# Row maxima over every second query, written to memory as two pieces of 16 bytes

## The chip, the cores and the metric

The kernel runs on one core of a Trainium2 chip. Its engines work side by side: TensorE (PE; its weight loads are listed apart, as PEld), VectorE (DVE), ScalarE (ACT), GpSimd (POOL) and the queue of SyncE (SP), which here issues nearly all transfers. The metric is the device time of one execution in microseconds, and a kernel's time is the median of several runs.

## What is computed

Two layers over x of 4 batches x 1024 tokens x 128 features. The change touches the attention of the first layer alone:

```python
qkv = X @ W_qkv                                   # 16 heads of 64, for q, k and v
q, k, v = (qkv[..., 0], qkv[..., 1], qkv[..., 2])
scores = jnp.einsum('bqhd,bkhd->bhqk', q, k) / scale
weights = jax.nn.softmax(scores, axis=-1)
attn = jnp.einsum('bhqk,bkhd->bqhd', weights, v)
return attn.reshape(b, s, h * d) @ W_out
```

A layer norm and a router of experts come ahead of it, the experts behind it, and then the second layer (a decaying recurrence and a gated network with weights rounded to 4 bits).

## The kernel before

Attention (`layer0_attention`) goes over N = 32 visits: 4 batches by 8 pairs of heads. The two heads of a pair lie on partitions 0 to 63 and 64 to 127 of `q_hi`, `k_hi` (the rounded parts of q and k) and `q_lo`, `k_lo` (the rests). The scores are made transposed: a tile has 128 keys as its partitions and the 512 queries of one half of the tokens, for both heads, as its columns. A visit has 16 steps t: half hf = t // 8, key tile kt = t % 8.

Softmax wants each query's maximum over all keys taken off ahead of the exponential. In the transposed tile a query is a column, and so the maxima come in another way:

- `row_max` on TensorE makes the scores once more, coarsely, the other way round: the queries are the stationary operand, 512 keys the moving one. One call is two matmuls, one for each head, into the bank pair `ps_m`. The 512 queries of a half are taken in four groups. A group is every fourth query, so the weight load (L1285) reads 128 fp32 columns of `q_hi` with a step of four elements, 16 bytes.
- `row_max` on VectorE (L1549) reduces `ps_m` to one maximum per query and head, in `mxh`. After eight such (4 groups by 2 halves of the keys) L1554 joins the key halves in `mx`: 8 numbers per partition.
- `spread` on the SP queue writes `mx` to the memory tensor `peaks` (L1169; a partition's 8 numbers, 32 bytes, are one run there), waits, and reads the 1024 numbers back to all 128 partitions, into `peak[hf]` (L1171).
- `seed` (L1455 on ScalarE; two steps of a visit, t = 3 and 15, L1681 on VectorE) writes minus the peak to a bank pair of `ps_s`, and `scores` (L1301, six matmuls a step: k_hi by q_hi, k_lo by q_hi, k_hi by q_lo, for two heads) adds upon it. L1471 takes the exponential on ScalarE into `probs`, a ring of 8; GpSimd adds the tiles up for the denominators (L1530).

All order is written out by hand. TensorE does two steps in a row, called a pair here, and each pair holds: row_max, the scores of the two steps, row_max, one item (a projection of K, Q or V for the next visit at L1232 to L1251, or an output projection, L1271), the products with V of two earlier steps (`values`, L1310) and, in two of the eight pairs of a visit, the sum for the denominators (L1260). `row_max` is 12 tiles ahead of the scores, so the eighth tile of a half is reduced at t = 3 or t = 11, and its peak is first wanted by the seed of t = 8 or of t = 0 of the next visit. `ps_m` is one bank pair: a call of row_max waits (m_done) for VectorE's reduction of the one before. ScalarE's pair is: two exponentials, the read of the item (L1418, L1424, or L1427 for a denominator), two seeds, and some small work (L1439 keep_values, L1409 stage, L1405, L1434). The seed of step t waits for the exponential of t - 2, which reads the same banks; `scores` waits for the seed.

Of the kernel before, what the change touches and what calls it, by code (L numbers as in the profile page):

```python
# [4 lines left out]
F32 = mybir.dt.float32  # L5
# [3 lines left out]
ALU = mybir.AluOpType  # L9
ACT = mybir.ActivationFunctionType  # L10
AX = mybir.AxisListType
# [3 lines left out]
P = 128  # L15
# [20 lines left out]
def attention_early(nc, ctx, g):  # L36

    sb, pb, sem = g.scope(ctx)
    g.qkv = sb("qkv_raw", [P, 3, PAIRS, 2 * DH], F32)
    g.wout = sb("wout_raw", [P, PAIRS, D], F32)  # L40
    g.w_hi = sb("w_hi", [P, 2, 2 * DH], F32R)
    g.w_lo = sb("w_lo", [P, 2, 2 * DH], F32R)
    g.wv_hi = sb("wv_hi", [P, PAIRS, 2 * DH], F32R)
    g.wv_lo = sb("wv_lo", [P, PAIRS, 2 * DH], F32R)
    g.wo = [sb("wo0", [P, D], F32), g.wo_last]
    g.probs = sb("probs", [P, RING, 2, CH], F32)
    g.psum_k = [sb(f"psum_k{h}", [P, 2, CH], F32) for h in range(2)]
    g.place = sb("place", [P, 2, TILES], U32)
    g.ones = sb("ones", [P, DH], F32)
    g.mx = sb("mx", [P, 4, 2], F32)  # L50
    g.V = [sb(f"V{p}", [P, TPB, 2 * DH], F32) for p in range(2)]

    spare = g.psum_k[0][:, :, :].rearrange("p x c -> p (x c)")
    g.top_i = spare[:, 0:256].bitcast(U32).rearrange("p (t e) -> p t e", e=E)
    g.carry = spare[:, 256:512].rearrange("p (e t) -> p e t", e=E)
    g.before = spare[:, 512:640]
    g.ones_n = spare[:, 640:768]
    g.ratio = spare[:, 768:768 + TILES]
    g.iota8 = spare[:, 800:800 + E]
    g.tile_no = spare[:, 808:808 + ROUTED]  # L60
    g.row_no = spare[:, 840:841]
    g.attn_w_in = sem("attn_w_in")
    g.preset = sem("preset")
    g.w_staged = sem("w_staged")
    g.wlo_staged = sem("wlo_staged")
    g.add_done = sem("add_done")
# [301 lines left out]
def load_rows(nc, sp, g, tile, s):  # L368

    dst = g.x_raw[s].rearrange("p (t d) -> p t d", d=ROW)  # L370
    sp.dma_start(dst, g.rows[bass.ds(tile * CH, CH), :].rearrange("(n p) d -> p n d", p=P)).then_inc(g.x_tile_in[s], 16)


def load_weights(nc, sp, g, first, w, s):

    sp.dma_start(w.bitcast(F32), g.w_split[bass.ds(first, P), :]).then_inc(g.w_tile_in[s], 16)
# [606 lines left out]
def layer0_attention(nc, ctx, g):  # L983

    sb, pb, sem = g.scope(ctx)
# [16 lines left out]
    probs, psum_k, ones, mx, V = g.probs, g.psum_k, g.ones, g.mx, g.V  # L1002
    w_in, preset, w_staged, wlo_staged, add_done = g.attn_w_in, g.preset, g.w_staged, g.wlo_staged, g.add_done
    even = [w[:, k * T:(k + 1) * T] for w in g.w_first for k in range(2)]
    k_hi, k_lo, q_hi, q_lo = ([even[k], sb(f"{name}1", [P, T], F32R)] for k, name in enumerate(("k_hi", "k_lo", "q_hi", "q_lo")))
# [5 lines left out]
    mxh = sb("mxh", [P, 2, 4, 2], F32)  # L1011
# [41 lines left out]
    mx_done = sem("mx_done")  # L1053
    mx_out = sem("mx_out")
# [47 lines left out]
    def max_bank(unit, i):  # L1102

        k = unit * KT + i if isinstance(unit, int) else KT + EARLY
        return ps_s[0] if k < KT + EARLY and k % 2 else ps_m

    def reads(n, name):

        c = READER[name]
        if n is None:  # L1110
            return sum(READER[k] == c for k in FIRST[:FIRST.index(name) + 1])
        if n is N:
            return N * PER[c] + AHEAD[c] + sum(READER[k] == c for k in LAST[:LAST.index(name) + 1])
        return n * PER[c] + AHEAD[c] + sum(READER[k] == c for k in LIST[:LIST.index(name) + 1])
# [32 lines left out]
    with nc.Block() as block:  # L1147
        @block.sync
        def _(sp):

            def move(p):

                sp.dma_start(V[p][:, :, :], V_next[:, :, p * 2 * DH:(p + 1) * 2 * DH]).then_inc(v_moved[p], 16)

            def expert_part(n):

                rows, col = bass.ds(n // QUARTERS * P, P), n % QUARTERS * QW
                sp.wait_ge(we_lo_done, n + 1)
                sp.dma_start(g.w_split[rows, bass.ds(col, QW)], we_hi[:, :].bitcast(F32)).then_inc(we_out, 16)
                sp.dma_start(g.w_split[rows, bass.ds(col + 2 * FF, QW)], we_lo[:, :].bitcast(F32)).then_inc(we_out, 16)  # L1160

            def load_part(n):

                sp.dma_start(we[:, :], g.inp["experts_d"][bass.ds(n // QUARTERS * P, P), bass.ds(n % QUARTERS * QW, QW)]).then_inc(we_in, 16)

            def spread(unit, hf):

                sp.wait_ge(mx_done, unit + 1)
                sp.dma_start(g.peaks[hf:hf + 1, :].rearrange("a (q k) -> q (a k)", k=8), mx[:, :, :].rearrange("p t x -> p (t x)")).then_inc(mx_out, 16)  # L1169
                sp.wait_ge(mx_out, unit * 16 + 16)  # L1170
                sp.dma_start(peak[hf][:, :, :].rearrange("p c x -> p (c x)"), g.peaks[hf:hf + 1, :].to_broadcast([P, 2 * CH])).then_inc(peak_in, 16)  # L1171

            load_part(0)
            spread(0, 0)
            sp.wait_ge(xa_done, AHEAD["a"])
            move(0)
            with sp.Fori(0, N // 2) as i:
                n = i * 2
                sp.wait_ge(v_ready, n * 2 + 1)
                move(1)  # L1180
                batch = bass.ds((n + 2) // PAIRS % B * T, T)
                sp.dma_start(xs_hi[:, :].bitcast(F32), g.xh[:, batch].bitcast(F32)).then_inc(xs_in, 16)
                sp.dma_start(xs_lo[:, :].bitcast(F32), g.xl[:, batch].bitcast(F32)).then_inc(xs_in, 16)
                spread(n * 2 + 1, 1)
                expert_part(n)
                load_part(n + 1)
                spread(n * 2 + 2, 0)
                spread(n * 2 + 3, 1)
                expert_part(n + 1)
                load_part((n + 2) % N)  # L1190
                spread(n * 2 + 4, 0)
                sp.wait_ge(xa_done, reads(n + 1, "V1"))
                move(0)
            sp.wait_ge(peak_in, (N * 2 + 1) * 16)
            sp.wait_ge(we_in, (N + 1) * 16)
            sp.wait_ge(we_out, N * 32)
            sp.wait_ge(v_moved[0], (N // 2 + 1) * 16)
            sp.wait_ge(scattered, 2 * TILES * 16)
            sp.wait_ge(routed, 2)
            load_rows(nc, sp, g, 0, 0)  # L1200
            sp.wait_ge(m_ready, KT + EARLY + N * STEPS)
            sp.wait_ge(xv_done, reads(N - 1, "Q1"))
            first = [sp.value_load(g.tile_w[0:1, s:s + 1], min_val=0, max_val=(E - 1) * P) for s in range(2)]
            load_weights(nc, sp, g, first[0], g.w_first[0][:, :], 0)
            load_rows(nc, sp, g, 1, 1)
            load_weights(nc, sp, g, first[1], g.w_first[1][:, :], 1)

        @block.tensor
        def _(pe):
# [64 lines left out]
            def row_max(unit, i, par, hf):  # L1274

                kh, t = divmod(i, 4)
                m = max_bank(unit, i)
                if m is ps_s[0] or isinstance(unit, int):
                    if unit * KT + i >= 2:
                        pe.wait_ge(m_done, unit * KT + i - 1)  # L1280
                else:
                    pe.wait_ge(m_done, unit * KT + i)
                q = q_hi[par][:, :].rearrange("p (c t) -> p t c", t=4)[:, t, hf * P:(hf + 1) * P]
                for x, rows in enumerate(HEADS):
                    ins = nc.tensor.matmul(m[:, x, :], q[rows, :], k_hi[par][rows, kh * CH:(kh + 1) * CH],  # L1285
                                           start=True, stop=True)
                ins.then_inc(m_ready, 1)
# [41 lines left out]
            def first_max(unit, *parts):  # L1329
                for i in parts:  # L1330
                    row_max(unit, i, 0, unit)
# [30 lines left out]
            for n, par in pairs(pe):  # L1362
                for t in range(STEPS):
                    p = t // 2
# [178 lines left out]
        def _(v):  # L1543
            def row_max(unit, i):
                kh, t = divmod(i, 4)
                v.wait_ge(m_ready, unit * KT + i + 1)
                if i == 0 and not (isinstance(unit, int) and unit == 0):
                    v.wait_ge(mx_done, unit)
                nc.vector.tensor_reduce(mxh[:, kh, t, :], max_bank(unit, i)[:, :, :], AX.X, ALU.max).then_inc(m_done, 1)  # L1549
                if i == KT - 1:  # L1550
                    v.wait_ge(m_done, unit * KT + KT)
                    if not (isinstance(unit, int) and unit == 0):
                        v.wait_ge(mx_out, unit * 16)
                    nc.vector.tensor_reduce(mx[:, :, :], mxh[:, :, :, :].rearrange("p k t x -> p t x k"), AX.X, ALU.max).then_inc(mx_done, 1)  # L1554

            def low(n, name, par):
                hi, lo = (k_hi, k_lo) if name[0] == "K" else (q_hi, q_lo)
# [939 lines left out]
```

## Time and profile before

| what | us |
|---|---|
| median of 3 runs | 1895.43 |
| lowest, highest | 1894.71, 1897.18 |
| the profiled execution | 1889.88 |
| its span, first to last instruction | 1888.0 |
| the attention's loop in it, about | 85 to 1485 |
| one visit in it | 43.78 |

The profiled execution is 5.5 us below the median. The profile gives, for an instruction, its start, its duration and, where its engine sat idle ahead of it, what ended that idle time. The ends of matmuls are modelled, so here starts are compared with starts. A weight load is a record of its own on PEld, and its matmul's record begins at the same moment where TensorE had stood still.

### The profile page before, as it was taken

To read this page: it belongs to the slowest core of one execution; us is meant where nothing else is said; L and a number is where in the kernel's file an instruction comes from. 1 tells how busy PE (TensorE), PEld (TensorE's weight loads), DVE (VectorE), ACT (ScalarE), POOL (GpSimd) and SP (SyncE) were. 2 spreads that over 40 slices of the span, in tenths; PEclk is the share of its full clock that TensorE was granted. 3 is DMA by queue.
4 is the path that set the end of the run, shared out by engine and by line. 5 is a ranking of instruction groups with operands and counts; after the bars stand their busy time and mean duration, and the time that the engine had idled before them with its cause. 6 is when DMAs were issued, how large, how long until landed. Compare 5 with 4: busy or idle time off the path is not lost. (4 is left out here: it accounts for less than half of the span.)

```text
span 1888.0 us, 32039 instructions
## 1 busy us (share of the span) xinstructions
PE 1785.0 (95%) x9247; PEld 989.1 (52%) x9247; DVE 1519.8 (80%) x2053; ACT 1464.2 (78%) x1954; POOL 1448.2 (77%) x868
## 2 busy tenths in 40 slices
PE   5799999999999999999999999999999899985687
PEld 4445444454454455554544544545445587763456
DVE  6787788888878777878878888778788788888896
ACT  4388888888888888888888888888888688874653
POOL 4288888888888888888888888888888457755564
PEclk9899999999999999999999999999999999997899
DMA  7112021212121121202121212112121577531000
GB/s 249 60 54 78 34 78 35 78 46 76 45 67 47 66 83 48 78 34 78 35 79 54 68 45 67 54 59 89 41 78 34 174 226 248 154 95 56 0 18 28
DMA packets 117014, 143.31 MB, mean 76 GB/s; under 512 B 18417, under 2 KB 98353, under 8 KB 113778
## 3 DMA queue, kind: packets, MB, share of 16 engines
q1 hardware_dynamic: 111986, 132.61, 22.4%
q0 software_dynamic: 4992, 10.27, 1.6%
q8 instruction: 16, 0.26, 0.1%
q14 instruction: 20, 0.16, 0.0%
HBM read 87.20 MB, written 27.64 MB: 61 GB/s over the span
## 5 line engine op out<-in xcount | busy, mean ns | idle before, releaser
L1530 POOL TENSOR_TENSOR psum_k<-psum_k,probs 128x1024 f32<-128x1024 f32 x384 | 929.9, 2422 | 144.8 <-ACT probs L1471 125.8
L1549 DVE TENSOR_REDUCE mxh<-ps_m 128x2 f32<-128x1024 f32 x518 | 623.6, 1204 | 242.7 <-PE ps_m L1285 242.6
L1471 ACT ACTIVATE probs<-ps_s 128x1024 f32<-128x1024 f32 x512 | 496.9, 1023 | 164.0 <-PE ps_s L1301 146.3
L1310 PE MATMUL ps_v<-probs,V 128*64 128x512 f32 x2056 | 494.6, 602 | 0.0
L1310 PEld LDWEIGHTS ps_v<-probs,V 128*64 128x64 f32 x2056 | 130.5, 136 | 239.2 <-issue 183.8
L1455 ACT ACTIVATE ps_s<-qkv_raw 128x1024 f32<-128x1024 f32 x224 | 243.6, 1124 | 0.0
L1455 ACT ACTIVATE ps_s<-peak 128x1024 f32<-128x1024 f32 x224 | 243.6, 1122 | 0.0
L1565 DVE RECIPROCAL e_y_row<-e_y_row 128x128 f32<-128x128 f32 x256 | 241.4, 943 | 0.0
L1530 POOL TENSOR_TENSOR psum_k<-probs 128x1024 f32<-128x1024 f32 x64 | 152.6, 2384 | 63.7 <-ACT probs L1471 47.7
L1301 PE MATMUL ps_s<-e_ew 64*128 64x512 f32 x1536 | 198.8, 390 | 0.0
L1285 PE MATMUL ps_m<-e_ew 64*128 64x512 f32 x524 | 163.9, 622 | 5.4 <-DVE mxh L1549 4.7
L1285 PEld LDWEIGHTS ps_m<-e_ew 64*128 64x128 f32 x524 | 80.9, 305 | 159.2 <-issue 104.6
L1301 PEld LDWEIGHTS ps_s<-e_ew 64*128 64x128 f32 x1536 | 146.3, 188 | 29.2 <-ACT ps_s L1455 2.4
L1285 PE MATMUL ps_m<-k_hi,q_hi 64*128 64x512 f32 x512 | 159.4, 619 | 0.0
L854 POOL DMA_INDIRECT results<-e_y_row,e_y_at x92 | 105.3, 1145 | 70.3 <-ACT e_y_row L795 43.4
L1285 PEld LDWEIGHTS ps_m<-k_hi,q_hi 64*128 64x128 f32 x512 | 79.0, 305 | 150.6 <-issue 103.8
L1301 PE MATMUL ps_s<-q_lo,k_hi 64*128 64x512 f32 x512 | 101.5, 392 | 0.0
L1301 PE MATMUL ps_s<-q_hi,k_lo 64*128 64x512 f32 x512 | 100.7, 389 | 0.0
L1301 PE MATMUL ps_s<-q_hi,k_hi 64*128 64x512 f32 x512 | 100.6, 389 | 0.0
L779 ACT ACTIVATE e_relu<-e_ps_z 128x512 f32<-128x512 f32 x124 | 74.6, 601 | 30.9 <-PE e_ps_z L708 28.3
L896 DVE TENSOR_TENSOR e_relu<-e_relu 128x512 f32<-128x512 f32 x108 | 74.5, 690 | 19.9 <-ACT e_relu L779 10.3
L900 DVE TENSOR_TENSOR e_h_lo<-e_relu,e_h_hi 128x512 fp32r<-128x512 f32 x124 | 88.4, 717 | 1.5 <-ACT e_h_hi L784 1.5
(317 smaller groups left out, 2918.0 us busy)
## 6 DMA issues: line engine op xcount, KB each, us to landing
e_ew<-w_split SPq DMA_DIRECT2D x23, 1024.0 KB
qkv_raw<-peaks SPq DMA_DIRECT2D x33, 512.0 KB, 3.9
V<-e_x_raw SPq DMA_DIRECT2D x33, 512.0 KB, 5.1
peak<-peaks SPq DMA_DIRECT2D x32, 512.0 KB, 4.1
xs_hi<-xh SPq DMA_DIRECT2D x16, 512.0 KB, 4.1
xs_lo<-xl SPq DMA_DIRECT2D x16, 512.0 KB, 5.0
rows<-in_blank_d SPq DMA_DIRECT2D x4, 1483.5 KB, 16.1
e_x_raw<-rows SPq DMA_DIRECT2D x23, 258.0 KB
```

The costliest lines, as they stand in the source:

```text
L779: nc.scalar.activation(r[:, q % NZ, :], ps_z[q % NZ][:, :], ACT.Relu).then_inc(relu_done, 1)
L854: nc.gpsimd.indirect_dma_start(g.results[:, :], bass.IndirectOffsetOnAxis(ap=y_at[s][:, t, 0:1], axis=0), y_row[s][:, t, :], None).then_in ...
L896: nc.vector.tensor_tensor(r2[:, q % NH, :], r[:, q % NZ, :], r[:, q % NZ, :], ALU.mult).then_inc(sq_done, 1)
L900: nc.vector.tensor_tensor(h_lo[:, q % NH, :], r2[:, q % NH, :], h_hi[:, q % NH, :].bitcast(F32), ALU.subtract).then_inc(lo_done, 1)
L1285: ins = nc.tensor.matmul(m[:, x, :], q[rows, :], k_hi[par][rows, kh * CH:(kh + 1) * CH], start=True, stop=True)
L1301: ins = nc.tensor.matmul(o[:, x, :], lhs[par][rows, keys], rhs[par][rows, qs], start=False, stop=True, skip_group_check=True)
L1310: ins = nc.tensor.matmul(ps_v[rows, :], V[par][:, kt, rows], probs[:, t % RING, x, :], start=kt == 0, stop=kt == KT - 1)
L1455: nc.scalar.activation(ps_s[t % 2][:, :, :], peak[hf][:, :, :].rearrange("p c x -> p x c"), ACT.Copy, scale=-1.0).then_inc(seeded, 1)
L1471: nc.scalar.activation(probs[:, t % RING, :, :], ps_s[t % 2][:, :, :], ACT.Exp, scale=SCALE).then_inc(p_done, 1)
L1530: nc.gpsimd.tensor_tensor(acc, probs[:, (t - 1) % RING, :, :] if kt == 1 else acc, probs[:, t % RING, :, :], ALU.add).then_inc(add_done, 1)
L1549: nc.vector.tensor_reduce(mxh[:, kh, t, :], max_bank(unit, i)[:, :, :], AX.X, ALU.max).then_inc(m_done, 1)
L1565: ins = nc.vector.reciprocal(rden[:, cols], den[:, cols])
```

## The change

The four groups of queries become two by two. The 512 queries of a half are split in two runs of 256 (s), and in each run a group is every second query (t). So L1285 loads 128 columns of `q_hi` with a step of two elements, 8 bytes, where it was four. `mx` holds the same 8 numbers per partition in the same order (group, head), named [s, t, x] now. Since the four numbers of s = 0 and those of s = 1 belong 2048 bytes apart in `peaks`, a partition's 32 bytes go there as two pieces of 16 bytes: 256 pieces where there were 128. `peaks` and `peak` look as before. Number, kind and order of the instructions on every engine stay the same.

```diff
-    g.mx = sb("mx", [P, 4, 2], F32)
+    g.mx = sb("mx", [P, 2, 2, 2], F32)
...
                 sp.wait_ge(mx_done, unit + 1)
-                sp.dma_start(g.peaks[hf:hf + 1, :].rearrange("a (q k) -> q (a k)", k=8), mx[:, :, :].rearrange("p t x -> p (t x)")).then_inc(mx_out, 16)
+                sp.dma_start(g.peaks[hf:hf + 1, :].rearrange("a (s q k) -> q (a s) k", s=2, k=4), mx[:, :, :, :].rearrange("p s t x -> p s (t x)")).then_inc(mx_out, 16)
...
-                q = q_hi[par][:, :].rearrange("p (c t) -> p t c", t=4)[:, t, hf * P:(hf + 1) * P]
+                two = hf * 2 + t // 2
+                q = q_hi[par][:, :].rearrange("p (c t) -> p t c", t=2)[:, t % 2, two * P:(two + 1) * P]
...
-                    nc.vector.tensor_reduce(mx[:, :, :], mxh[:, :, :, :].rearrange("p k t x -> p t x k"), AX.X, ALU.max).then_inc(mx_done, 1)
+                    nc.vector.tensor_reduce(mx[:, :, :, :].rearrange("p s t x -> p (s t) x"), mxh[:, :, :, :].rearrange("p k t x -> p t x k"), AX.X, ALU.max).then_inc(mx_done, 1)
```

## Rows read from the trace of the kernel before

**Rows 1.** The attention's loop by engine: stretch, length, busy us, PEclk, DMA share.
```profile
85.00:1485.00 1400.00, 1399.67 (x7420) 697.85 (x7418) 1121.75 (x1184) 1171.32 (x1376) 1194.82 (x640) 1.00 0.19 61
```

**Rows 2.** TensorE's matmuls in time: start, us, line, tiles, number merged.
```profile
792.98 0.62 PE L1285 MATMUL ps_m<-k_hi,q_hi 64*128 64x512 f32 x2
...
803.52 0.63 PE L1285 MATMUL ps_m<-k_hi,q_hi 64*128 64x512 f32 x2
803.99 1.54 PE L1301 MATMUL ps_s<-e_ew 64*128 64x512 f32 x12
805.47 0.63 PE L1285 MATMUL ps_m<-k_hi,q_hi 64*128 64x512 f32 x2
806.03 0.50 PE L1232 MATMUL ps_x<-xh,w_hi 128*128 x1
806.37 0.40 PE L1233 MATMUL ps_x<-xl,w_hi 128*128 x1
...
809.66 0.62 PE L1285 MATMUL ps_m<-k_hi,q_hi 64*128 64x512 f32 x2
...
814.93 0.63 PE L1285 MATMUL ps_m<-k_hi,q_hi 64*128 64x512 f32 x2
...
836.76 0.62 PE L1285 MATMUL ps_m<-e_ew 64*128 64x512 f32 x2
```

**Rows 3.** Weight loads of two lines over the whole span: ns min/median/max.
```profile
L1285 PEld LDWEIGHTS ps_m<-e_ew x524: 304/305/309, 49.7 to 1478.3; 64*128 64x128 f32 x175
...
L1301 PEld LDWEIGHTS ps_s<-e_ew x1536: 182/184/332, 81.7 to 1434.0; 64*128 64x128 f32 x192
```

**Rows 4.** Weight loads ahead of the loop, in time.
```profile
63.07 0.31 PEld L1285 LDWEIGHTS ps_m<-e_ew 64*128 64x128 f32 x2 [3.08 <-DVE mxh L1549]
...
65.33 0.33 PEld L1251 LDWEIGHTS ps_x<-wv_hi,xl 128*128 128x128 f32 x1
...
69.43 0.19 PEld L1250 LDWEIGHTS ps_v<-wv_lo,xh 128*128 128x128 f32 x1
```

**Rows 5.** Weight loads of the scores in the loop, in time; idle time in brackets.
```profile
799.29 0.56 PEld L1301 LDWEIGHTS ps_s<-e_ew 64*128 64x128 f32 x6 [0.15 <-ACT ps_s L1455]
...
830.64 0.31 PEld L1285 LDWEIGHTS ps_m<-k_hi,q_hi 64*128 64x128 f32 x2 [0.81 <-issue]
...
831.57 0.19 PEld L1301 LDWEIGHTS ps_s<-q_hi,k_hi 64*128 64x128 f32 x2
```

**Rows 6.** ScalarE in time.
```profile
804.96 1.94 ACT L1471 ACTIVATE probs<-ps_s 128x1024 f32<-128x1024 f32 x2 [0.56 <-PE ps_s L1301]
807.04 0.60 ACT L1418 ACTIVATE q_hi<-ps_x 128x512 fp32r<-128x512 f32 x1
...
809.94 0.60 ACT L1439 ACTIVATE e_y_row<-ps_v 128x512 f32<-128x512 f32 x1 [0.22 <-DVE e_y_row L1578]
...
811.11 1.94 ACT L1471 ACTIVATE probs<-ps_s 128x1024 f32<-128x1024 f32 x2
...
813.66 2.12 ACT L1455 ACTIVATE ps_s<-peak 128x1024 f32<-128x1024 f32 x2
...
821.60 1.94 ACT L1471 ACTIVATE probs<-ps_s 128x1024 f32<-128x1024 f32 x2 [2.25 <-PE ps_s L1301]
...
824.14 2.17 ACT L1455 ACTIVATE ps_s<-qkv_raw 128x1024 f32<-128x1024 f32 x2
```

**Rows 7.** VectorE in time, the reductions of ps_m.
```profile
804.20 1.23 DVE L1549 TENSOR_REDUCE mxh<-ps_m 128x2 f32<-128x1024 f32 x1 [1.11 <-PE ps_m L1285]
...
831.31 1.23 DVE L1549 TENSOR_REDUCE mxh<-ps_m 128x2 f32<-128x1024 f32 x1 [0.21 <-PE ps_m L1285]
```

**Rows 8.** The SP queue in time, one spread.
```profile
813.82 0.33 SPq L1169 DMA_DIRECT2D peaks<-mx  x1
815.23 0.32 SPq L1171 DMA_DIRECT2D qkv_raw<-peaks  x1
```

**Rows 9.** From issue to landing: first the writes of L1169, then the reads of L1171.
```profile
DMA to landing us min/median/max: 1.4/1.4/2.6
...
DMA to landing us min/median/max: 3.3/4.0/4.4
```

## The prediction

> **What bounds the kernel now.** I read first the busy times of the attention's loop, since nothing outside it changes but 12 row maxima ahead of it. In its 1400 us TensorE has a matmul in flight all the time, at a granted clock of 1.00, while POOL is busy for 1195, ACT for 1171 and DVE for 1122 us [rows 1]. A busy PE alone proves little, as ends of matmuls are modelled, so the second view is TensorE in order of time [rows 2]. Two things are to be seen there. The visit repeats after 836.76 - 792.98 = 43.78 us; 32 of them are 1401 us. And inside a pair each record begins a fixed time behind the one before: no gap on TensorE is left that another engine fills. The three others do wait: ACT sits idle 0.56 us ahead of the exponentials of an ordinary pair, for the scores [rows 6], and DVE 1.11 us or less ahead of a first reduction, for `ps_m` [rows 7]. So TensorE's own sequence sets the pace, and what its instructions cost one behind the other is what a visit costs.
>
> One place looks like a tie. The second row_max of a pair starts at 805.47 [rows 2], and DVE ends the reduction it waits for at 804.20 + 1.23 = 805.43 [rows 7]. But the twelve score records from 803.99 on need till then as well (1.54 us, whose modelled end is 805.53). Both limits hang on the first row_max, and both would move with it.
>
> **The weight load: where a gain can come from.** The load of L1285 takes 305 ns, with hardly a spread; the load of the scores, also 64 x 128, takes 184 ns at the median [rows 3]. They differ in the step through memory, 16 bytes against 4. Rows 4 show what kind of cost that is. Ahead of the loop, at the lower of TensorE's two clock levels, the dense load takes 0.33 us, and later 0.19; the stepped load takes 0.31 us there too. The dense load follows the clock, the stepped one does not: it is held by the read.
>
> Is the load on the path? TensorE puts the matmul behind its own load when a new kind of work starts. From a row_max to the score record behind it are 803.99 - 803.52 = 0.47 us; from the first matmul of a projection, loaded densely, to its second are 806.37 - 806.03 = 0.34 us, with the same 512 moving columns [rows 2]. The difference, 0.13, is the difference of the loads, 0.12. So the whole load difference stands on the path, once per row_max (the two heads load at the same time, on different partitions). The same holds at the second row_max: 0.56 us to the load of the item.
>
> **What the load costs at a step of two.** The trace has no such load. Its bounds are 184 ns (dense) and 305 ns (step of four); nothing in the rows lets it be faster than dense or slower than step four. I take 184. [...] If it goes by the element, whenever neighbours aren't read together, it stays 305. [...] No row here shows a step of two, so the bounds above stay.
>
> Sum on TensorE: 305 - 184 = 121 ns a row_max, two in a pair, 0.24 us a pair; 16 in a visit are 1.94 us; 512 in the loop are 62 us. The 12 ahead of the loop wait for DVE and give nothing.
>
> **What is late next: ScalarE.** The exponentials' start in a pair moves only 0.12 (one row_max lies ahead of it), the pair shortens by 0.24, and ACT's work stays. TensorE's pair of 5.27 (809.66 to 814.93) becomes 5.03, and the longer one of 6.14 (803.52 to 809.66) becomes 5.90 [rows 2]. The load for the scores of a pair's second step starts 831.57 - 830.64 = 0.93 after the pair [rows 5], 0.81 then, and it needs the second seed.
>
> Ordinary pair: from the start of the exponentials to the end of the second seed are 824.14 + 2.17 - 821.60 = 4.71 us [rows 6]. The exponentials begin 1.44 after the pair (804.96 - 803.52), 1.32 then. The seed is ready at 1.32 + 4.71 = 6.03, less about 0.1 since the item is ready earlier and ACT goes straight on: 5.93. Wanted at 5.03 + 0.81 = 5.84. A hold of 0.1; but the load is well ahead of its matmul: where it was held for 0.15 [rows 5], the pair kept its length. So nothing or a few hundredths.
>
> The pair behind the first denominators is worse. From 804.96 to the exponentials at 811.11 are 6.15 us, and no idle time for TensorE's scores is left there: item, seeds, keep_values behind DVE's product at 809.94, denominator, exponential [rows 6]. TensorE would want 5.90. So they start 0.25 late, at 1.45 - 0.12 + 0.25 = 1.58 after the pair; the seeds end at 813.66 + 2.12 - 811.11 = 4.67 later, less 0.05: 6.20 against 5.84. Held 0.36, of which at least 0.11 is absorbed: 0.15 to 0.25 lost. The pair after it has a single seed and 2.25 us of idle time on ACT (821.60), so it ends there.
>
> I take 0.25 us a visit for all of this, bounds 0 and 0.7: 8 us, 0 to 22.
>
> DVE: its idle time ahead of a first reduction is 0.21 at the least [rows 7] and shrinks by 0.12, as its work begins 0.12 earlier and is wanted 0.24 earlier; it stays above nothing. POOL: 1195 of 1400 us [rows 1], that is 37.3 us of a visit that would have 42, with a ring of 8 tiles between; no cost. The reductions and the small join keep their sizes: no cost.
>
> **The write in 16-byte pieces.** L1169 is issued at 813.82, and the read back at 815.23 [rows 8]; a write lands after 1.4 us and a read after at most 4.4 [rows 9]: the peak is there by 819.6. The seed that wants it starts at 824.14 [rows 6]. 4.5 us of cover, about 4.0 when the two pairs between are shorter. Doubling the pieces could at worst double the 1.4. Cost nothing; it would begin to cost when a write takes more than 5.4 us. [...]
>
> **The sum.** -62 + 8 = -54 us. Against the profiled execution: 1889.9 - 54 = 1836; it lies 5.5 below the median, so for the median 1895.4 - 54 = 1841.
>
> **Rivals.**
> 1. The load goes by the element and stays 305 ns: nothing on the path changes, 1895. For it: only two steps are in the trace. Against it: the clock's absence from the load. 0.12. That the change doesn't do what it says is the same case.
> 2. The load falls half way, to some 245 ns: 512 x 0.06 = 31 us less, and ACT isn't reached: 1865. 0.10. [...]
> 3. Full load gain, but ScalarE takes 0.7 us a visit: 62 - 22 = 40, 1855. This lies in the forecast's own range.
> 4. Slower: the pieces. If a write took 7.5 us, the peak would be late by 7.5 - 5.4 = 2.1 us at each of 64 spreads, ACT and behind it TensorE would stand: 134 - 54 = 80 us slower, 1975. It turns to a loss above 5.4 + 54/64 = 6.2 us, over four times the 1.4 of now. 0.05.
>
> **How the numbers follow.** Forecast 0.73, its own range 1828 (0.13 at each of 512, no loss: 67 us) to 1855. Load half way 0.10, none 0.12, slower 0.05. The range that holds 8 in 10 reaches from 1828 over the half-way case to 1880. A measurement of this kernel tells 0.2%, some 4 us, from no change. Faster by more: 0.83; within: 0.12; slower: 0.05.
>
> **What would show it.** Load of L1285 near 185 ns; row_max to score record 0.34 in place of 0.47; the ordinary pair near 5.03 and the longer one near 5.90; the visit near 42.1; ACT's idle time ahead of the exponentials down to about 0.4 in an ordinary pair, and the load of L1301 held by the seed in the pair after the denominators; landing of L1169 below 3 us. I am wrong if the load stays at 305, or if it falls and the visit doesn't.

## The result, and the profile after

| | before | changed |
|---|---|---|
| median, us | 1896.31 (4 runs) | 1844.62 (4 runs) |
| lowest, highest | 1894.71, 1897.26 | 1841.06, 1851.33 |
| span of the profiled execution | 1888.0 | 1839.2 |

The ratio is 0.9732, with a 95% interval of 0.9703 to 0.9761: 2.7% faster, some 51 us. The forecast was 1841, with a range of 1828 to 1880.

The weight loads of the row maxima in the changed kernel (ns min/median/max), which answer to [rows 3]; L1286 is what L1285 was:

```profile
L1286 PEld LDWEIGHTS ps_m<-e_ew x524: 189/191/287, 49.6 to 1426.1; 64*128 64x128 f32 x175
...
L1286 PEld LDWEIGHTS ps_m<-k_hi,q_hi x512: 189/191/192, 91.7 to 1394.2; 64*128 64x128 f32 x171
```

305 ns have become 191. TensorE in time, the pair behind the first denominators and the four after it (start, us, line, tiles), which answer to [rows 2]:

```profile
782.01 0.51 PE L1286 MATMUL ps_m<-k_hi,q_hi 64*128 64x512 f32 x2
782.36 1.56 PE L1302 MATMUL ps_s<-e_ew 64*128 64x512 f32 x12
...
787.05 0.51 PE L1286 MATMUL ps_m<-k_hi,q_hi 64*128 64x512 f32 x2
...
792.04 0.51 PE L1286 MATMUL ps_m<-k_hi,q_hi 64*128 64x512 f32 x2
...
797.12 0.51 PE L1286 MATMUL ps_m<-k_hi,q_hi 64*128 64x512 f32 x2
...
799.16 0.51 PE L1286 MATMUL ps_m<-k_hi,q_hi 64*128 64x512 f32 x2
...
802.32 0.51 PE L1286 MATMUL ps_m<-k_hi,q_hi 64*128 64x512 f32 x2
...
824.14 0.50 PE L1286 MATMUL ps_m<-e_ew 64*128 64x512 f32 x2
```

From a row_max to the score record behind it are 782.36 - 782.01 = 0.35 us, where it was 0.47. The visit is 824.14 - 782.01 = 42.13 us, where it was 43.78. The starts of these loads give the length of every pair in both traces; the medians over the 32 visits:

| pair | 0 | 1 | 2 | 3 | 4 | 5 | 6 | 7 | visit |
|---|---|---|---|---|---|---|---|---|---|
| before | 5.22 | 6.12 | 5.27 | 5.26 | 6.12 | 5.27 | 5.22 | 5.26 | 43.75 |
| changed | 5.20 | 5.88 | 5.04 | 5.03 | 5.89 | 5.03 | 4.99 | 5.08 | 42.15 |

Here pair 0 is the pair of steps 0 and 1 of a visit; the pair from 782.01 on, behind the first denominators, is pair 5. Six pairs got 0.23 or 0.24 shorter, as two row maxima at 0.12 would have it. Pair 7 got 0.18 and pair 0 only 0.02. The visit lost 1.60 us, 32 of them 51 us: the whole result. The question left is what became of pair 0.

The waits in 200 to 1400 us of the changed kernel (who waited for whom, total, times, longest) show how close the other engines have come:

```profile
DVE mxh L1550 <- PE ps_m L1286: 151.8, 198, 1.3
ACT probs L1472 <- PE ps_s L1302: 114.5, 172, 2.0
...
PEld ps_s L1302 <- ACT ps_s L1456: 18.4, 101, 0.3
```

The last line is the loads of the scores held by ScalarE's seed; in the kernel before it was:

```profile
PEld ps_s L1301 <- ACT ps_s L1455: 1.9, 12, 0.2
```

And the landing of the write in two pieces, then of the read back, against 1.4/1.4/2.6 and 3.3/4.0/4.4 in [rows 9]:

```profile
DMA to landing us min/median/max: 1.5/2.4/4.3
...
DMA to landing us min/median/max: 3.4/4.2/4.7
```

### The profile page after: what moved, and what is told of

Its sections match the earlier page's. It is cut to its first block and busy times, and to the rows that moved or that the text cites. A ratio compares the mean times of both kernels' runs of the same rounds, so it can differ in the third digit from the quotient of the medians.

```text
span 1839.2 us, 32039 instructions
## 1 busy us (share of the span) xinstructions
PE 1730.6 (94%) x9247; PEld 923.6 (50%) x9247; DVE 1542.1 (84%) x2053; ACT 1458.5 (79%) x1954; POOL 1448.6 (79%) x868
## 5 line engine op out<-in xcount | busy, mean ns | idle before, releaser
L1302 PEld LDWEIGHTS ps_s<-e_ew 64*128 64x128 f32 x1536 | 140.9, 185 | 33.7 <-ACT ps_s L1456 11.3
L1286 PE MATMUL ps_m<-e_ew 64*128 64x512 f32 x524 | 133.5, 506 | 8.7 <-DVE mxh L1550 6.1
L1286 PEld LDWEIGHTS ps_m<-e_ew 64*128 64x128 f32 x524 | 51.2, 192 | 163.4 <-issue 107.3
L1286 PE MATMUL ps_m<-k_hi,q_hi 64*128 64x512 f32 x512 | 129.4, 502 | 2.1 <-DVE mxh L1550 0.2
L1286 PEld LDWEIGHTS ps_m<-k_hi,q_hi 64*128 64x128 f32 x512 | 49.7, 191 | 152.1 <-issue 103.9
L1579 DVE TENSOR_TENSOR e_y_row<-e_y_row 128x512 f32<-128x512 f32 x64 | 100.5, 1570 | 0.0
```

What stands on the lines that cost most here:

```text
L1302: ins = nc.tensor.matmul(o[:, x, :], lhs[par][rows, keys], rhs[par][rows, qs], start=False, stop=True, skip_group_check=True)
L1579: nc.vector.tensor_tensor(attn[:, :], raw[:, :], rden[:, :], ALU.mult).then_inc(attn_done, 1)
```

## Is it the load, and the load alone?

The write, without the load:

```diff
-    SCALE = DH ** -0.5
+    SCALE = 2.0 ** -20
...
-                sp.dma_start(g.peaks[hf:hf + 1, :].rearrange("a (q k) -> q (a k)", k=8), mx[:, :, :].rearrange("p t x -> p (t x)")).then_inc(mx_out, 16)
+                sp.dma_start(g.peaks[hf:hf + 1, :].rearrange("a (s q k) -> q (a s) k", s=2, k=4), mx[:, :, :].rearrange("p (s t) x -> p s (t x)", s=2)).then_inc(mx_out, 16)
```

> The kernel before with the write of the maxima alone changed: 256 pieces of 16 bytes, the weight load of the row maxima still with a step of four. The pieces land in places that don't belong to their queries, and the exponential's scale is set to 2^-20 so that nothing overflows; sizes and order are as before. My theory (the gain is all the weight load's, the write is covered): no change, within 0.2%, visit 43.75 us, load 305 ns, landing of the write 2.4 us as in the changed kernel. Rival (the write's landing, 1 us later, costs part of what the load gives): slower by up to 64 x 1.0 = 64 us, or a visit up to 2 us longer.

Measured: ratio to the kernel before 1.000, interval 0.9977 to 1.0023; visit 43.75 us, every pair within 0.01 of before; load 305 ns. The landing of the write, in this kernel:

```profile
DMA to landing us min/median/max: 1.5/2.3/3.7
```

So the median write does land a microsecond later, and the visit isn't longer by a hundredth.

The load, without the write:

```diff
-    SCALE = DH ** -0.5
+    SCALE = 2.0 ** -20
...
-                sp.dma_start(g.peaks[hf:hf + 1, :].rearrange("a (s q k) -> q (a s) k", s=2, k=4), mx[:, :, :, :].rearrange("p s t x -> p s (t x)")).then_inc(mx_out, 16)
+                sp.dma_start(g.peaks[hf:hf + 1, :].rearrange("a (q k) -> q (a k)", k=8), mx[:, :, :, :].rearrange("p s t x -> p (s t x)")).then_inc(mx_out, 16)
```

> The changed kernel with the write of the maxima put back: one piece of 32 bytes per partition, the weight load with a step of two. The maxima land in places that don't belong to their queries, the exponential's scale is 2^-20. My theory: as the changed kernel, ratio to the kernel before 0.973, visit 42.15 us, load 191 ns, landing 1.4 us. Rival (the smaller pieces cost some of the gain): faster than the changed kernel, ratio 0.970 or below.

Measured: ratio 0.973 (0.9688 to 0.9772), visit 42.15 us, load 191 ns, landing 1.4 us; its pairs are those of the changed kernel to 0.01. The two parts add up, and the load is the whole.

## What the step of a weight load costs

```diff
-    SCALE = DH ** -0.5
+    SCALE = 2.0 ** -20
...
-                two = hf * 2 + t // 2
-                q = q_hi[par][:, :].rearrange("p (c t) -> p t c", t=2)[:, t % 2, two * P:(two + 1) * P]
+                half = q_hi[par][:, hf * CH:(hf + 1) * CH]
+                q = (half[:, 0:P],
+                     half[:, 0:2 * P].rearrange("p (c t) -> p t c", t=2)[:, 0, :],
+                     half[:, 0:3 * P].rearrange("p (c t) -> p t c", t=3)[:, 0, :],
+                     q_hi[par][:, :].rearrange("p (c t) -> p t c", t=8)[:, 0, :] if hf
+                     else half.rearrange("p (c t) -> p t c", t=4)[:, 0, :])[t]
```

> The changed kernel with a different step for the weight load of each of the four groups: 1, 2 and 3 elements, and for the fourth 8 where the second half of the tokens is worked on, 4 otherwise. The maxima are not those of their queries, the exponential's scale is 2^-20. [...] Theory B (time goes by 16-byte lines touched; step 4 and step 8 both touch one line per element): step 3, which touches 96 lines for 128 elements, about 245, step 8 305 ns. Theory C (what counts is whether each line gives two elements): step 3 anywhere between 191 and 305, step 8 305.

This kernel ran once, so its trace is used and its total is not. The five loads, told apart by their place in the order (median over the loop; the lines of 16 bytes that 128 elements touch are worked out from the step):

| step, elements | 1 | 2 | 3 | 4 | 8 |
|---|---|---|---|---|---|
| load, ns | 183 | 191 | 248 | 305 | 308 |
| lines touched | 32 | 64 | 96 | 128 | 128 |

Some of them in the trace (weight loads of `ps_m`, in time, steps 3, 4 or 8, 1, 2, 3):

```profile
799.42 0.25 PEld L1290 LDWEIGHTS ps_m<-k_hi,q_hi 64*128 64x128 f32 x2 [0.81 <-issue]
...
801.30 0.31 PEld L1290 LDWEIGHTS ps_m<-k_hi,q_hi 64*128 64x128 f32 x2 [0.37 <-DVE mxh L1554]
...
804.62 0.18 PEld L1290 LDWEIGHTS ps_m<-k_hi,q_hi 64*128 64x128 f32 x2 [0.81 <-issue]
...
806.44 0.20 PEld L1290 LDWEIGHTS ps_m<-k_hi,q_hi 64*128 64x128 f32 x2 [0.34 <-DVE mxh L1554]
...
809.61 0.25 PEld L1290 LDWEIGHTS ps_m<-k_hi,q_hi 64*128 64x128 f32 x2 [0.81 <-issue]
```

The time doesn't go by the stretch of memory passed over: a step of 8 passes over twice as much as one of 4 and takes 1% more, where the line through 191 and 305 would have it at 533 ns. Theory B holds and theory C isn't needed: from 64 lines on each 32 lines add 57 ns, 1.8 ns a line, and 305 less twice 57 is 191. The size of a line comes out of the steps too: lines of 8 bytes would make steps 2, 3 and 4 alike, and lines of 32 bytes would make a step of 8 dearer than one of 4. Below 64 lines something else holds the load, at 183. That floor is higher at the clock's lower level. Where the granted clock is at its lower level (0.50, ahead of the loop, 58 to 68 us in the changed kernel), a load at a step of two that follows no other directly takes 283 to 286 ns, and the dense one of the next kernel 283 to 285 at that level. At a step of four, in the kernel before, it takes 306 there (at 72.95 and 81.51 us), as in the loop. (At 49.6 and 52.3 us of the changed kernel the load at a step of two takes 282 to 287 ns too, where the profile lists 1.00.) So the time goes by lines of 16 bytes touched, above a floor of 183 ns in the loop, at a clock of 1.00, and of 283 to 285 at 0.50. A step of two, with two elements to a line, lies 8 ns above the dense load.

The same run shows what a load is worth on the path. Its pair 1 works on the third and fourth group: loads of 248 and 305 ns against two of 191, 0.171 us more. That pair took 6.06 us, against 5.88 in the changed kernel. Its pair 2, with 183 and 191, took 5.03 against 5.04. Pairs 3 and 5 got 0.18 and 0.17 longer, so load time and pair time go one to one; only pair 7 gave 0.12, which is taken up below.

A dense load throughout, with the maxima written as four pieces of 8 bytes (`mx` is [P, 4, 2] again, as before the change):

```diff
-                two = hf * 2 + t // 2
-                q = q_hi[par][:, :].rearrange("p (c t) -> p t c", t=2)[:, t % 2, two * P:(two + 1) * P]
+                q = q_hi[par][:, hf * CH + t * P:hf * CH + (t + 1) * P]
...
-                sp.dma_start(g.peaks[hf:hf + 1, :].rearrange("a (s q k) -> q (a s) k", s=2, k=4), mx[:, :, :, :].rearrange("p s t x -> p s (t x)")).then_inc(mx_out, 16)
+                sp.dma_start(g.peaks[hf:hf + 1, :].rearrange("a (s q k) -> q (a s) k", s=4, k=2), mx[:, :, :]).then_inc(mx_out, 16)
```

> The changed kernel one step further: a group is 128 neighbouring queries, the weight load dense, and a partition's maxima go to memory as four pieces of 8 bytes, 512 pieces. It computes what the reference does. My theory: the load falls from 191 to 184 ns, 512 x 7 ns = 3.6 us at most; the write lands later (1.4 with 128 pieces, 2.4 with 256, so about 4.4 with 512), with the cover of some 4.9 us between the end of the spread and the seed before the change it is still hidden. Ratio to the kernel before 0.971 to 0.973. Rival (the cover is used up): seeds wait for the peak, the ratio is above 0.975.

Measured: ratio 0.9712 (0.9670 to 0.9755), load 183 ns, visit 42.09 us. The difference to the changed kernel is 0.06 us a visit, 2 us in all: in the traces, and below what these runs' totals tell apart. The write in 512 pieces:

```profile
DMA to landing us min/median/max: 2.9/4.0/5.5
```

1.4, 2.4 and 4.0 us at the median for 128, 256 and 512 pieces of the same 4 KB. The visit doesn't show it.

## What became of pair 0

In the changed kernel the second row_max of pair 0 starts 799.16 - 797.12 = 2.04 us after the first; in the other pairs it is 1.82. Two things precede it. The load of the scores of that pair is held by ScalarE's seed, and the reduction that the row_max waits for starts late. Weight loads, then VectorE, in the changed kernel:

```profile
797.11 0.19 PEld L1286 LDWEIGHTS ps_m<-k_hi,q_hi 64*128 64x128 f32 x2 [0.81 <-issue]
...
798.07 0.18 PEld L1302 LDWEIGHTS ps_s<-q_hi,k_hi 64*128 64x128 f32 x2 [0.18 <-ACT ps_s L1456]
...
799.15 0.19 PEld L1286 LDWEIGHTS ps_m<-k_hi,q_hi 64*128 64x128 f32 x2 [0.56 <-DVE mxh L1550]
```

```profile
795.98 0.69 DVE L1560 TENSOR_TENSOR e_ew<-ps_x,e_ew 128x512 fp32r<-128x512 f32 x1 [0.23 <-ACT e_ew L1419]
796.59 1.37 DVE L1579 TENSOR_TENSOR e_y_row<-e_y_row 128x512 f32<-128x512 f32 x1
797.89 1.21 DVE L1550 TENSOR_REDUCE mxh<-ps_m 128x2 f32<-128x1024 f32 x1
```

In every other pair the first reduction starts 0.55 us after its row_max; here that would be 797.67. But it starts at 797.89, has no idle time ahead of it, and ends at 799.10; the row_max follows at 799.15. Ahead of it stands the product of raw and rden (L1579), which takes 1.37 us. In the kernel before, the same product took 0.82, and the reduction behind it had to wait for TensorE:

```profile
826.08 1.22 DVE L1549 TENSOR_REDUCE mxh<-ps_m 128x2 f32<-128x1024 f32 x1 [0.36 <-PE ps_m L1285]
```

GpSimd at that moment, in the changed kernel:

```profile
795.04 2.38 POOL L1531 TENSOR_TENSOR psum_k<-psum_k,probs 128x1024 f32<-128x1024 f32 x1
```

and in the kernel before, with the product beside it:

```profile
822.78 2.38 POOL L1530 TENSOR_TENSOR psum_k<-psum_k,probs 128x1024 f32<-128x1024 f32 x1
...
824.89 0.82 DVE L1578 TENSOR_TENSOR e_y_row<-e_y_row 128x512 f32<-128x512 f32 x1
```

Both products end 0.54 to 0.55 us after GpSimd's addition: 796.59 + 1.37 = 797.96 against 797.42, and 825.71 against 825.16. It holds at all 64 products of each of the two traces: each meets an addition and ends 0.546 to 0.556 us after it, however long its record is, 0.8 to 1.8 us. From this I estimate that some 0.55 is the product's own part, and that the rest is a wait for the addition to end. (No run has this product without an addition beside it.) The other way round, the addition behind it takes 2.68 to 2.74 us where 2.39 is usual.

Why the wait grew: GpSimd does four additions in a row there, back to back, at its own pace (10.18 us before, 10.11 after), while TensorE, ScalarE and VectorE have come nearer together by the pairs that got shorter. The product comes 796.59 - 789.41 = 7.18 us after GpSimd's L71 now; it was 824.89 - 817.11 = 7.78. It meets the addition earlier in its run and waits, by that estimate, 0.83 us where it waited 0.27. Two other kernels fit in. In the one with mixed steps this product took 1.10 us, the reduction behind it wasn't late, and pair 0 had its full gain, at 4.98; with the dense loads it took 1.40, and pair 0 stood at 5.22.

Take the product away:

```diff
-                nc.vector.tensor_tensor(attn[:, :], raw[:, :], rden[:, :], ALU.mult).then_inc(attn_done, 1)
+                if hf:
+                    nc.vector.tensor_tensor(attn[:, :], raw[:, :], rden[:, :], ALU.mult).then_inc(attn_done, 1)
+                else:
+                    nc.vector.memset(attn[:, :], 1.0).then_inc(attn_done, 1)
```

> The changed kernel, in which VectorE fills attn with ones for the second output of a visit (half 0) where it multiplied raw by rden; that multiplication is left out. It tells what holds the first pair of a visit, which got only 0.02 us shorter (5.22 to 5.20) where the others got 0.24. Theory A: the product waits on VectorE for GpSimd's running addition to end (1.37 us in place of 0.82), the next reduction of ps_m starts late and the second row_max of that pair with it; then the pair falls to 5.00, the visit from 42.15 to 41.95, some 6 us in all. Theory B: the pair is held by ScalarE's seed for its second step (the load of the scores sits idle 0.18 us there); then it stays at 5.20, or gives 0.04 at most.

Measured: ratio 0.9708 (0.9693 to 0.9723), pair 0 4.99 us, visit 41.94, the other pairs unchanged. The place in the trace:

```profile
794.50 0.48 DVE L1582 MEMSET e_y_row<- 128x512 f32 x1
795.42 1.22 DVE L1550 TENSOR_REDUCE mxh<-ps_m 128x2 f32<-128x1024 f32 x1 [0.45 <-PE ps_m L1286]
```

```profile
795.82 0.19 PEld L1302 LDWEIGHTS ps_s<-q_hi,k_hi 64*128 64x128 f32 x2 [0.18 <-ACT ps_s L1456]
796.70 0.20 PEld L1286 LDWEIGHTS ps_m<-k_hi,q_hi 64*128 64x128 f32 x2 [0.35 <-DVE mxh L1550]
```

The load of the scores is still held for 0.18 us by the seed, and the pair has its full gain: theory B falls, and this hold costs nothing. Theory A stands.

Keep the product, but put it where a wait does no harm:

```diff
                 inverse(n, 0, 3)
+                normalise(n, 0)
                 step(15)
                 low(n, "K0", par)
-                normalise(n, 0)
```

> The changed kernel with VectorE's product for half 0 moved ahead of the last reduction and the low part of K0, so that a wait for GpSimd ends earlier and in front of work that isn't wanted so soon. It computes what the reference does. Theory A (the product's wait for GpSimd delays the reduction that TensorE needs): first pair of a visit from 5.20 to about 5.00, ratio to the kernel before 0.970 or a little below. Theory B (ScalarE's seed holds the pair): no change, 0.973. A loss would show if the last reduction of the visit, which then starts up to 1.4 us later, is late for the row_max behind it.

Measured: ratio 0.9698 (0.9685 to 0.9711), pair 0 4.99 us, visit 41.92. VectorE there:

```profile
793.13 0.80 DVE L1579 TENSOR_TENSOR e_y_row<-e_y_row 128x512 f32<-128x512 f32 x1
793.85 1.21 DVE L1550 TENSOR_REDUCE mxh<-ps_m 128x2 f32<-128x1024 f32 x1
794.98 0.67 DVE L1560 TENSOR_TENSOR e_ew<-ps_x,e_ew 128x512 fp32r<-128x512 f32 x1
796.08 1.22 DVE L1550 TENSOR_REDUCE mxh<-ps_m 128x2 f32<-128x1024 f32 x1 [0.43 <-PE ps_m L1286]
```

The reduction that TensorE waits for has 0.43 us of idle time ahead of it again.

The changed kernel ran beside it:

> The changed kernel itself, once more, beside the three others on the same chip: ratio 0.973, visit 42.15 us.

Measured: ratio 0.9747 (0.9732 to 0.9763), a little above the 0.973 expected; visit 42.14 us, as expected, pair 0 5.20. In one group of runs the product moved takes 1830.85 us at the median and the changed kernel 1837.52; by the visits it is 32 x 0.22 = 7 us.

Both steps together:

> Both steps together: dense loads with 8-byte pieces, and the product earlier. It computes what the reference does. Expected: 2 to 3 us less than with the product earlier alone, ratio 0.968 to 0.970, if the write in 512 pieces stays covered.

Measured: ratio 0.9684 (0.9670 to 0.9697), median 1828.22, visit 41.85 us. It is the fastest of all, 3.2% below the kernel before. Against the product moved alone, 0.07 us a visit are 2 us; the intervals of the two overlap.

## Why the prediction was right, point by point

**What bounds the kernel.** Right. TensorE's sequence set the pace, and outside pairs 0 and 7 load time turned into pair time one to one, in both directions (191 ns, and 248 and 305 put back).

**The load at a step of two.** Right in size: 184 was taken, 191 came. No run shows the 184 ns that the sum of 62 us takes for a step of two: it was my estimate, set at the dense load's figure, and the loads of the changed kernel showed 191 in its place. Nor does the time go by the element, as the first rival had it: the steps of 1, 2, 3, 4 and 8 show that it goes by lines touched. [rows 4] do not show the level of the clock that the reading needed: the profile lists a granted clock of 1.00 for 60 to 67 us, though the dense load takes 0.33 us there. It lists 0.50 from 72.62 to 82.86 us, and in there a load of L1285 took 0.31 us (at 72.95) and a dense one of L1233 took 0.33 (at 76.62), so that reading holds. Taken by the loads the sum would be 114 ns a row_max, and 512 of them 58 us; the pairs gave 0.235 for two, 60 us. The term of 62 us was 2 to 4 too large.

**ScalarE late next.** Wrong: 8 us were put down for it, and no run shows it to cost anything. The step that failed is the reading of the 6.15 us between two exponentials as ScalarE's own work. In the changed kernel that stretch reads:

```profile
819.58 1.94 ACT L1472 ACTIVATE probs<-ps_s 128x1024 f32<-128x1024 f32 x2 [0.45 <-PE ps_s L1302]
...
824.57 0.60 ACT L1440 ACTIVATE e_y_row<-ps_v 128x512 f32<-128x512 f32 x1 [0.36 <-DVE e_y_row L1579]
825.07 0.59 ACT L1428 ACTIVATE e_y_row<-ps_x 128x512 f32<-128x512 f32 x1
825.54 1.95 ACT L1472 ACTIVATE probs<-ps_s 128x1024 f32<-128x1024 f32 x2
```

825.54 - 819.58 = 5.96 us. The 0.19 more of before were a wait for TensorE's scores at its end, too short to be listed as idle time: from the denominator's read to the exponential were 811.11 - 810.43 = 0.68 us, now 825.54 - 825.07 = 0.47. And even the 5.96 isn't all ScalarE's: 0.36 of it is a wait for VectorE's product. So the exponentials start 825.54 - 824.14 = 1.40 us after the pair, where 1.58 was forecast, and pair 5 got its full 0.24. The hold of 0.36 us that was forecast in it did not come; its loads of the scores run through without idle time:

```profile
782.13 1.36 PEld L1302 LDWEIGHTS ps_s<-e_ew 64*128 64x128 f32 x12
```

Holds by the seed came in pairs 0, 3, 4 and 6 instead, 0.16 to 0.21 us at the median and 18.4 us in all in 200 to 1400 us. Pairs 3, 4 and 6 have their full gain in spite of them, and so has pair 0 once the product is taken away. That a hold of 0.1 to 0.2 us costs nothing or a few hundredths was right.

**VectorE and GpSimd: no cost.** This is where the 0.28 us a visit went that are missing to eight pairs at 0.235. I took the product's 0.82 us for its size, when 0.27 of it was, by the estimate above, a wait for GpSimd, and looked at GpSimd's busy share but not at where its additions lie beside VectorE's products. VectorE's cover, 0.36 us at the reduction that was hit and 0.21 at the least, would have held for an instruction that keeps its length; this one got 0.55 longer. Pair 0 lost 0.21 us by it, which moving the product gave back. Pair 7 lost 0.05 us otherwise: the load of the item K0 comes 0.48 us after the second row_max, where other items come after 0.44. With the loads of 248 and 306 ns put back, it comes after 0.55 like the others, and so pair 7 got only 0.12 longer there: something beside the load takes 0.48 us, and a longer load hides it. What it is, no run shows.

**The write.** Right that it is covered. Its size wasn't: "at worst double the 1.4" met a median of 2.4 and a highest of 4.3, where the landing was to stay below 3. For this write from the SP queue, measured are 1.0 us more for 128 more pieces and 2.6 more for 384, 7 to 8 ns a piece.

**The sum.** 62 - 8 = 54 was forecast, 51 measured: a gross gain of 60, and a loss of 9 where I had none. 7 of the 9 are pair 0's, from VectorE and GpSimd, and some 2 are pair 7's. That the 8 us put on ScalarE come near this 9 is luck: the sum came out near by it, and without it 62 would have stood against 51. The totals also tell less than was said, some 0.3% either way instead of 0.2%.

## What to carry to other kernels

Here, wherever TensorE changed over to a row_max, its weight load stood bare on the path (0.17 us more of load made pairs 1, 3 and 5 of the run with mixed steps 0.17 to 0.18 us longer). Where a trace shows that, let the load read at least two fp32 of every 16 bytes (191 ns here, against 305 with one), and put the cost of the other layout where a transfer is covered. After any gain on one engine look where an engine that keeps its own pace (here GpSimd's additions) now lies beside the others' instructions: the records of VectorE's product, 0.8 to 1.8 us, were by my estimate 0.55 of work and the rest a wait, and that wait changed when the schedule did. A stretch between two instructions of an engine that is said to bound it should be added up from its pieces, not taken as a difference of starts.

## What the runs showed of the hardware that I had not expected

- The weight load of `ps_m` goes by 16-byte lines touched, 1.8 ns each from 64 lines on, and a step of 8 elements costs no more than one of 4 (308 and 305 ns).
- VectorE's product ends 0.55 us after the end of GpSimd's addition at all 64 of the kernel before and all 64 of the changed one, however long its record is, 0.8 to 1.8 us; what lies above 0.55 is inside the record and isn't listed as idle time.
- A write of 4 KB lands after 1.4, 2.4 and 4.0 us in 128, 256 and 512 pieces, and with 256 pieces its highest is 4.3.
- What comes behind the loop is the noisier part: from the start of the last product with V to the end were 403.8 us in the profile of before, 412.7 in that of `pieces_only`, and 406.7 and 401.4 in two profiles of the changed kernel, while the visits agree to 0.01 us. For a change in the loop the visit is the better measure.
